# Cross-attention and feed-forward block: the turn of the largest scores, VectorE's statistics and the low halves of x change their places

## The reference, cut to what matters

```
h      = layernorm(x)                                  # x: (16, 512, 512)
q      = rope(split(h @ Wq))                           # 16 heads of 32
k, v   = rope(split(ctx @ Wk)), split(ctx @ Wv)        # ctx: (16, 120, 512)
attn   = softmax(q @ k.T / sqrt(32))
x1     = x + merge(attn @ v) @ Wo
scale  = max(abs(layernorm(x1))) / 32767               # act_qdq needs one maximum over all of it
out    = x1 + ffn(layernorm(x1))                       # 4-bit weights, 16-bit activations
```

## Time and profile before

| what | value |
|---|---|
| time, median of 3 runs | 2372.98 us (2372.72 to 2377.24) |
| the profiled execution's own time | 2381.01 us |
| its span in the profile | 2378.9 us |
| TensorE matmuls (PE) | 2245.7 us busy, 94% |
| VectorE (DVE) | 1679.1 us, 71% |
| ScalarE (ACT) | 1284.7 us, 54% |
| GpSimd (POOL) | 703.6 us, 30% |

### The profile page before, as it was taken

The page is one execution under the profiler, slowest core; times in us unless marked ns, Lnnn a source line. Parts: engine busy times, 40 slices in busy tenths (PEclk is TensorE's granted clock), DMA queues, the critical chain, the costliest instruction groups (busy, mean ns, idle before and its releaser), DMA issues. The chain is left out here.

```text
span 2378.9 us, 32353 instructions
## 1 busy us (share of the span) xinstructions
PE 2245.7 (94%) x12869; PEld 1013.1 (43%) x12869; DVE 1679.1 (71%) x1702; ACT 1284.7 (54%) x1195; POOL 703.6 (30%) x493
## 2 busy tenths in 40 slices
PE   5898999989998899999999999999999599999999
PEld 3443444434443344444444444444444244444444
DVE  6555888788876657545543489888888777777774
ACT  3345554545443223222322588778876677777772
POOL 3454666656654311000100155444444000000000
PEclk9899999999999999999999999999999799999999
DMA  6333565555667558778875798777777465555552
GB/s 189 91 105 111 170 175 165 163 168 168 183 155 164 136 175 258 256 250 263 264 244 182 217 369 299 286 282 283 283 287 286 160 243 214 211 211 213 215 228 88
DMA packets 286712, 500.20 MB, mean 210 GB/s; under 512 B 187500, under 2 KB 189804, under 8 KB 249692
## 3 DMA queue, kind: packets, MB, share of 16 engines
q1 hardware_dynamic: 286556, 498.09, 64.1%
HBM read 247.75 MB, written 186.58 MB: 183 GB/s over the span
## 5 line engine op out<-in xcount | busy, mean ns | idle before, releaser
L1609 PE MATMUL banks<-XB,WT 128*128 128x512 f16 x2304 | 499.0, 380 | 4.0 <-ACT OB L1629 4.0
L1609 PE MATMUL banks<-XB,W 128*128 128x512 f16 x2304 | 500.4, 381 | 2.3 <-ACT XB L1635 2.3
L2057 PE MATMUL banks<-W,OH 128*128 128x512 f16 x2256 | 489.4, 380 | 7.1 <-DVE OH L2151 7.1
L1629 ACT ACTIVATE OB<-banks,uns 128x512 f32<-128x512 f32 x384 | 255.1, 684 | 394.5 <-PE banks L1609 389.2
L1609 PEld LDWEIGHTS banks<-XB,WT 128*128 128x128 f16 x2304 | 225.7, 98 | 277.2 <-ACT OB L1629 4.4
L1609 PEld LDWEIGHTS banks<-XB,W 128*128 128x128 f16 x2304 | 226.0, 98 | 276.2 <-issue 5.3
L2057 PEld LDWEIGHTS banks<-W,OH 128*128 128x128 f16 x2256 | 221.2, 98 | 275.3 <-DVE OH L2151 7.6
L1891 POOL TENSOR_TENSOR PR<-GS,OB 128x2048 f32<-128x2048 f32 x46 | 221.0, 4805 | 262.6 <-ACT OB L1629 242.2
L1718 DVE TENSOR_REDUCE amx<-OB 128x1 f32<-128x2048 f32 x48 | 109.7, 2285 | 239.2 <-ACT OB L1629 239.2
L922 ACT ACTIVATE P<-banks 120x2048 f32<-120x2048 f32 x60 | 112.3, 1872 | 154.0 <-PE banks L652 153.9
L721 PE MATMUL banks<-XC,AH 128*128 128x512 f16 x768 | 181.5, 388 | 3.9 <-POOL AH L1419 3.9
(11 more groups left out here) (266 smaller groups left out, 2928.8 us busy)
## 6 DMA issues: line engine op xcount, KB each, us to landing
g_s<-OB SPq DMA_DIRECT2D x48, 1024.0 KB, 5.9
GL<-g_s SPq DMA_DIRECT2D x48, 1024.0 KB, 8.2
up_s<-OB SPq DMA_DIRECT2D x48, 1024.0 KB, 4.9
XA<-up_s SPq DMA_DIRECT2D x32, 1024.0 KB, 9.4
gq_s<-GQ SPq DMA_DIRECT2D x48, 512.0 KB, 5.2
XD<-gq_s SPq DMA_DIRECT2D x48, 512.0 KB, 6.7
XA<-in_x SPq DMA_DIRECT2D x16, 1024.0 KB, 7.7
QW<-QE SPq DMA_DIRECT2D x128, 128.0 KB, 2.9
```

Of the source, the lines that this page charges most:

```text
L1609: t = e.matmul(pk[:].rearrange("p (j t) -> p j t", j=4), WT[w][:, ot, wa, kk, :], XB[i % 2][:, xa, :, kk, :], start=(kk == 0 and wa == 0 a ...
L1629: e.activation(OB[n % 3][:, r, :], bank[(k + 4) % 8][:], ACT.Copy, scale=uns[:, 12 * w + ot:12 * w + ot + 1]).then_inc(s_ev, 1)
L2057: t = e.matmul(pk[:].rearrange("p (r n) -> p r n", r=4), OH[i % 2][:, a, ot, j * 128:(j + 1) * 128], WD[:, :, c, wa, o4, :], start=(ot == ...
```

## The change

Four edits, in the lists of four engines:

- TensorE: the turn of the largest scores at c = 2 goes behind the other key and value passes and behind the output projection. In `pe_scores` the four matmuls L649 go ahead of the wait for MT.
- ScalarE: the eviction to MT goes ahead of the two AH evictions from step 16 on, and behind the key and value evictions before step 16.
- VectorE: the statistics of x1 go right behind x1, ahead of the rotary sum, the reciprocals and the maximum. From step 17 on the low half of x goes from the end of c = 1 to the next step, behind these statistics.
- SP: from step 17 on the x turn is issued a step later, at c = 2, behind that step's swap.

```diff
@@ sp_attention
-                for nb in [1] if s == 2 else x_at(s, 2):
+                for nb in [1] if s == 2 else x_at(s, 2) if s < 16 else x_at(s - 1, 2) if s > 16 else []:
                     sp_x_turn(e, nb)
@@ pe_scores
+            for g in range(4):
+                e.matmul(PB[0:SK, g, :], KR[g0][32 * g:32 * g + 32, c, bb * SK:(bb + 1) * SK], QR[u % 8][32 * g:32 * g + 32, :],
+                         start=True, stop=False)
             if c == 0:
                 e.wait_ge(s_mte, b + 1)
             if u == 0:
                 e.wait_ge(s_sel, 2)
-            for g in range(4):
-                e.matmul(PB[0:SK, g, :], ...)
@@ pe_attention
-                if c == 2 and 0 <= b - 1 < B:
-                    pe_turn_largest(e, b - 1)
                 for i in kv[1:]:
                     pe_kv(e, i, s)
                 for u in output_at(s):
                     pe_output(e, u)
+                if c == 2 and 0 <= b - 1 < B:
+                    pe_turn_largest(e, b - 1)
@@ act_attention
+        def act_largest(e, b):
+            e.wait_ge(s_mt, b + 1)
+            if b >= 1:
+                e.wait_ge(s_c1, 4 * (b - 1) + 4)
+            e.activation(MT[:], BQ_, ACT.Copy, scale=1.0 / MS).then_inc(s_mte, 1)
...
                 for i in kv[:1]:
                     act_kv(e, i)
+                if c == 2 and 0 <= b - 1 < B and s >= 16:
+                    act_largest(e, b - 1)
                 for u in normal_at(s):
...
-                if c == 2 and 0 <= b - 1 < B:
-                    e.wait_ge(s_mt, b)
-                    ...
-                    e.activation(MT[:], BQ_, ACT.Copy, scale=1.0 / MS).then_inc(s_mte, 1)
                 for i in kv[1:]:
                     act_kv(e, i)
+                if c == 2 and b >= 1 and s < 16:
+                    act_largest(e, b - 1)
@@ dve_attention
                 for u in output_at(s - 1):
                     dve_x1(e, u)
+                for u in output_at(s - 1):
+                    dve_x1_stats(e, u)
+                for nb in x_at(s - 1, 2) if s > 16 else []:
+                    dve_x_low(e, nb)
...
-                for u in output_at(s - 1):
-                    dve_x1_stats(e, u)
                 if s in (11, 12):
                     dve_amax(e, {11: 7, 12: 8}[s])
...
-                for nb in [1] if s == 2 else x_at(s, 2):
+                for nb in [1] if s == 2 else x_at(s, 2) if s < 16 else []:
                     dve_x_low(e, nb)
```

More of the change, by code:

```diff
@@ L647, in pe_scores @@
                 e.wait_ge(s_sel, 2)
-            for g in range(4):
-                e.matmul(PB[0:SK, g, :], KR[g0][32 * g:32 * g + 32, c, bb * SK:(bb + 1) * SK], QR[u % 8][32 * g:32 * g + 32, :],
-                         start=True, stop=False)
             for g in range(4):
@@ L957, in act_attention @@
                     e.activation(AH[nb % 2][:, 0, nc_, :], A[:, u % 6, :], ACT.Copy).then_inc(s_ah, 1)
-                if c == 2 and 0 <= b - 1 < B:
-                    e.wait_ge(s_mt, b)
-                    if b >= 2:
-                        e.wait_ge(s_c1, 4 * (b - 2) + 4)
-                    e.activation(MT[:], BQ_, ACT.Copy, scale=1.0 / MS).then_inc(s_mte, 1)
                 for i in kv[1:]:
                     act_kv(e, i)
+                if c == 2 and b >= 1 and s < 16:
+                    act_largest(e, b - 1)
                 if s in (4, 6):
```

## The result

The changed kernel takes 2385.43 us (median of ten, 2380.22 to 2390.35), the kernel before 2373.81 (ten, 2372.72 to 2379.45): a ratio of 1.0043, 95% interval 1.0032 to 1.0054. It is slower by 0.4%, some 10 us. The profiled execution of the changed kernel took 2384.83 us with a span of 2382.7, at its own median; that of the kernel before took 2381.01, some 7 above its median.

| starts at, us | before | after |
|---|---|---|
| transpose that ends the attention (L838) | 834.9 | 844.5 |
| transpose that ends gate and up (L2075; after: L2083) | 1861.1 | 1865.8 |
| span | 2378.9 | 2382.7 |

A forecast was written before the change was run, and what follows sets the result against it. TensorE, busy 94% of the span, was taken as the bound. Terms +6.0 - 3.6 - 0.6 - 0.3 + 2.2 = +3.7 us moved the median 2372.98 to 2376.7; own range 2371 to 2382, wide range 2358 to 2389.

The forecast's parts named there:

- c = 2: Attention steps with s mod 4 = 2: new wait for the maximum; 11.1 against 11.0 us, +0.1 per batch.
- c = 1: Attention steps with s mod 4 = 1: normalising x ahead of the exponential in every batch; +0.3 us per batch.
- likeliest case: Whole kernel: slightly slower, +3.7 us to 2376.7, MT and QE waits replaced by maximum and x1 waits; chance 0.45.
- B: Rival: faster, 2357 us, as GpSimd's sine and low halves don't meet VectorE's weight preparation; chance 0.27.
- D: Rival: no gain or loss, 2373 us; start-up delay is taken up and waits only change names; chance 0.10.
- C: Rival: slower, 2390 us; later reciprocals delay RB, high halves and the exponential where s mod 4 = 2; chance 0.18.
- c = 3: Attention steps with s mod 4 = 3: output matmuls wait 0.8 us for x1; 10.4 against 10.23, +0.2 per batch.
- ten batches: Attention steps 18 to 57, four steps per batch: +0.6 us each, +6 in all.
- steps 58 to 63: Late attention steps: output matmuls fill the wait for QE, late x1 costs 0.8; together -3.6 us, bounds -5 and 0.
- steps 66, 67: Last attention steps: the wait behind MT goes at step 66, where no maximum follows the turn; -0.6 us.
- start-up, to step 8: From step 6, the turn behind two key passes delays scores, maximum and what follows; +2.2 us, bounds 0 and 2.5.
- Step 62: Late attention step: output matmuls run during the wait for QE, scores 2.98 us behind the turn; 13.0 us long.

The follow-up runs named there:

- e2_recip: Changed kernel with the statistics of x1 put behind the reciprocals in steps with s mod 4 = 0; 2376.70 us, ratio 1.0005.
- e11_turn_levels: Kernel before with only TensorE's and ScalarE's edits, plus the two level products moved behind x1; 2377.99 us, ratio 1.0022.
- e6_levels: Changed kernel with the two level products of each weight tile moved behind x1; 2368.52 us, ratio 0.9975.
- e9_short: Changed kernel with the level products of twelve weight tiles cut from 512 to 32 columns; one run, 2367.7 us, only the attention to be read.
- e4_lists: Kernel before with only VectorE's and SP's edits; 2372.59 us, ratio 0.9994.
- e7_mt_first: e4_lists with MT evicted ahead of the AH evictions from step 16 on, turn at its old place; 2368.51 us, ratio 0.9982.
- e8_mt_recip: e7_mt_first with the statistics of x1 behind the reciprocals in steps with s mod 4 = 0; 2361.33 us, ratio 0.9943.
- e12_again: The same kernel as e8_mt_recip, run once more; 2361.46 us, ratio 0.9943.
- e1_start: Changed kernel with the turn and ScalarE's eviction to MT at their old places before step 16; 2383.65 us, ratio 1.0031.
- e5_turn: Kernel before with only TensorE's and ScalarE's edits; 2379.26 us, ratio 1.0018.

## Why the prediction was right, and where its sizes were off

The likeliest case held in its mechanism: waits for MT and QE replaced by waits for the maximum and for x1, and not B (faster) or D. In size it did not: forecast 2376.7 us with its own range of 2371 to 2382, measured 2385.4, which only the wide range holds. A forecast of +3.7 us lay inside the 4.7 that it took for "no change"; the measured +0.43% is slower and clear of noise. By the time alone C, at 2390, was nearer than the forecast, and the repair of C's chain in e2_recip gives back most of the loss; that C's own sign (waits of over 1 us for the exponential at c = 2) showed up only once, in step 42, is what speaks against it. The sum, +3.7, meets the +3.8 between the two profiles by luck, as the stages show: the attention grew by 9.5. Step by step:

| part | forecast, us | measured, us |
|---|---|---|
| c = 2 against before, per batch | +0.1 | -0.18 |
| c = 3 | +0.2 | +0.85 |
| c = 0 | 0 | 0 |
| c = 1 | +0.3 | -0.22 |
| ten batches | +6 | +4.6 |
| steps 58 to 63 | -3.6 | -1.4 |
| steps 66, 67 | -0.6 | -0.7, +5.1 |
| start-up, to step 8 | +2.2 | +2.3 (counted inside a run +2.5) |
| steps 8 to 17 | -0.3 | +0.7 |

The measured parts come to 10.5 us by the start of step 70; the last matmuls behind it give back 0.9.

- *c = 2* was right: turn to scores is 2.92 us at step 34 (437.88 to 440.80) against the 2.98 of the earlier trace rows, and the wait is 0.5 us ten times. Of the 0.3 for late exponentials 0.2 came, in steps 42 and 50.
- *c = 3* is the term that was mis-sized: +0.85 instead of +0.2. L721 waited 1.2 us per batch, not 0.8, because x1 began at 5.7 us on the mean of steps 23 to 55 and 6.0 at step 35, not at 5.2. The stretch of the two products was priced well (1.7 us; 1.6 at step 35). What was left out are the short scalings ahead of them, which are stretched too: L1176 took 1.12 us at step 35 and 0.17 at step 43 of e11_turn_levels, L1184 0.61 and 0.23. The sum also priced a wait at its own length, while at step 35 the matmuls behind it took 1.69 us longer as well. e6_levels and e9_short show that x1's lateness is the cause; The prediction had the products meet GpSimd's passes because the turn makes them late; e4_lists shows the same stretch with the turn at its old place. (It also read six late maxima off, where there are five.)
- *c = 1* was expected to grow, because ScalarE would normalise x ahead of its exponential in every batch. The waits did become regular (0.4 us in nearly every batch), but they are shorter than the old ones, 3.4 us in sum against 5.4, and the step became shorter.
- *The reciprocals' chain*, rival C, had its 0.3 in the forecast at c = 2. It is real: undoing it gave 9 us in e2_recip and 7 from e7_mt_first to e8_mt_recip. In e2_recip it acted at c = 2, as C had it, by 2 us in ten batches, and for the greater part (7 us) through GpSimd's position at c = 3, a way that the prediction hadn't seen.
- *Step 62* took 14.9 us, not 13.0. QE came later in the step than before (the turn started 11.2 us into it, not 10.0), so the turn waited 3.32 us more behind the output matmuls, and the scores followed 3.75 us behind it instead of 2.98. That is 1.9 of the missing 2.2 us; step 59 was 0.6 longer than forecast, and step 63 paid 0.55, less than the 0.8 forecast.
- *Step 67* was not foreseen at all, and is the largest error of a single step. Read from the trace, the store of x1 stands ahead in SP's queue, so late x1 makes the sums, the reciprocals (3.0 us into step 64 instead of 1.0) and their broadcast to RB late, then GpSimd's products and low halves. No experiment shows this chain: in e6_levels the reciprocals also stand at 3.0, and step 67 is 6.40. One step alone misleads here, too: e12_again has 11.25 and e8_mt_recip, the same program, 6.75, but in e12_again steps 64 and 65 were 3.2 us shorter. Steps 64 to 67 together took 36.8 us before and 41.1 in the changed kernel, e1_start and e2_recip: 4.3 more. In e5_turn it is 2.9 more, and in every version with the products moved or shortened, or the turn at its old place, at most 1.5 (e12_again). That points to VectorE's list, late under the moved turn, as the root; the path from there to the low halves stays open.
- *Start-up* was right in size, by distances inside a run; e1_start shows that turn and MT account for all of it up to step 7 and for 1.1 of the 2.5 us up to step 8.

## What to carry over

An edit that pins one instruction in an in-order list moves all that stands behind it, so ask first which work of the other engines now lies on the same microseconds. One edit can stretch a piece of work and another take away the slack in which the stretch was free: each passes alone, the pair doesn't. Price them together, against the moment when the result is due, and run the halves apart when the sum disagrees. Look also at the drain of the pipeline, where short steps no longer hide what the long ones did.

## What the runs showed of the hardware

- Beside two GpSimd passes, two VectorE products of 128x512 took 1.44 and 1.53 us instead of 0.69 each, and GpSimd's pair 2.73 instead of the 2.27 of step 67; cut to 128x32, the products took 0.95 and 1.08.
- A wait of 1.69 us of TensorE was followed by twelve matmuls in 4.45 us at a granted clock of 0.62, instead of 2.76 (step 35). At step 16 the same twelve (L670) took 4.45 behind a wait of 1.77 in the changed kernel, and ran at full speed behind one of 1.87 in the kernel before. In the changed kernel's own steps 27 and 51 waits of 1.68 and 1.67 were followed by 2.76 (granted clock 1.00). The price of such a wait is not fixed.
- One DMA transpose held SP's queue for 4.97 us (438.37).
- A stretch that no edit touches (gate and up) differed by up to 6 us between the profiled executions (1020.5 to 1026.2), as much as most single edits here are worth.
